# The chunked gated delta rule: the second value head with its two batches exchanged between the halves of the partitions

## The reference, cut to what matters

```
q,k,v,z = x @ W_qkvz;  q,k,v through a causal convolution of 4 taps and silu;  q,k normalized
attn    = inverse of (1 + strictly lower part of (beta k k^T * decay))          # 64x64 per chunk
v_prime = attn @ (v beta) - (attn @ (k beta exp g)) @ state
out     = (q exp g) @ state + (lower part of q k^T * decay) @ v_prime
state   = state * exp(g_last) + (k decay)^T @ v_prime                          # 128x128
result += rmsnorm(out * silu(z)) @ W_out[head]
```

## Time and profile before

| | |
|---|---|
| median of 3 runs | 4948.56 us (4940.16 to 4948.61) |
| the profiled execution | 4963.24 us, its span 4961.4 us |
| granted clock of PE, mean | 0.984 |
| PE busy | 4639.9 us, 94% |
| DVE busy | 3576.3 us, 72% |
| ACT busy | 3063.8 us, 62% |
| POOL busy | 693.1 us, 14% |
| DMA | 305.22 MB, 62 GB/s |

### The profile page before, as it was taken

How to read it: one execution, slowest core, us unless ns; L and a number is a source line. 1 busy time by engine, 2 the same in 40 slices (tenths; PEclk the granted TensorE clock), 3 DMA queues, 4 the chain that set the end, 5 groups by cost and what they waited for, 6 DMA issues and landing times.

```text
span 4961.4 us, 144941 instructions
## 1 busy us (share of the span) xinstructions
PE 4639.9 (94%) x54288; PEld 3178.9 (64%) x54320; DVE 3576.3 (72%) x7576; ACT 3063.8 (62%) x7979; POOL 693.1 (14%) x680
## 2 busy tenths in 40 slices
PE   4898999999999899999999899999999999999998
PEld 2555666666666566666666666666666666666666
DVE  7554777777777677777777677777777777777776
ACT  2333666666666566666666566666666666666665
POOL 0000111111111111111111111111111111111111
PEclk8999999999999999999999999999999999999999
DMA  2111222222223222222223222222223232222221
GB/s 61 32 43 60 66 69 52 61 67 61 68 50 81 69 68 50 64 67 61 59 58 81 68 58 59 64 63 65 60 57 81 68 69 55 59 66 60 69 58 34
DMA packets 760100, 305.22 MB, mean 62 GB/s; under 512 B 672880, under 2 KB 716016, under 8 KB 749168
## 3 DMA queue, kind: packets, MB, share of 16 engines
q1 hardware_dynamic: 620144, 287.40, 23.6%
q10 hardware_dynamic: 139264, 8.42, 1.8%
HBM read 216.96 MB, written 66.07 MB: 57 GB/s over the span
## 4 chain that ended last, share of the span: by engine, by line
PE 71%; DVE 8%; ACT 6%; issue 6%; SPq 5%; DMA 4%; ACTq 0%; DVEq 0%; POOL 0%; POOLq 0%
PE pj L660 16%; PE dsb L819 8%; PE pj L655 7%; PE pod L803 4%; PE pot L777 4%; PE dsb L791 4%; PE ms L693 4%; PE pot L748 4%; PE pod L760 3%; PE pj L650 3%; ACT arena L983 2%; PE pot L605 2%; PE ms L673 2%; SPq L333 2%; PE ms L687 2%
## 5 line engine op out<-in xcount | busy, mean ns | idle before, releaser
L660 PE MATMUL pj<-xnT,wt 128*128 128x512 f32 x2048 | 1023.2, 623 | 29.3 <-DMA cw<-in_L_attn_conv_weight 15.7
L1292 DVE SCALAR_TENSOR_TENSOR cy<-xpad,cw,cy 128x1024 f32<-128x1024 f32 x768 | 981.3, 1278 | 10.4 <-ACT cy L1003 1.2
L1562 POOL TENSOR_TENSOR rout<-rin,expo 128x2 f32<-128x2 f32 x512 | 358.3, 700 | 3743.4 <-DVE rin L1443 3743.4
L819 PE MATMUL dsb<-wo,yT 128*128 128x256 f32 x2048 | 575.7, 404 | 17.9 <-issue 16.9
L660 PEld LDWEIGHTS pj<-xnT,wt 128*128 128x128 f32 x2048 | 352.2, 192 | 358.9 <-issue 343.9
L1429 DVE SCALAR_TENSOR_TENSOR st<-st,gel,dsb 128x128 f32<-128x128 f32 x1536 | 430.4, 343 | 207.7 <-PE dsb L791 202.8
L1002 ACT ACTIVATE xpad<-pj 128x512 f32<-128x512 f32 x512 | 304.9, 596 | 360.8 <-PE pj L660 360.8
L655 PE MATMUL pj<-wt,xnT 128*128 128x256 f32 x2048 | 510.0, 392 | 0.0
L1062 ACT ACTIVATE yT<-dsb 128x256 f32<-128x256 f32 x512 | 202.2, 395 | 491.2 <-PE dsb L810 489.5
L819 PEld LDWEIGHTS dsb<-wo,yT 128*128 128x128 f32 x2048 | 348.7, 190 | 123.2 <-issue 95.4
L655 PEld LDWEIGHTS pj<-wt,xnT 128*128 128x128 f32 x2048 | 368.9, 190 | 84.0 <-issue 44.3
(11 more groups left out here) (174 smaller groups left out, 8011.6 us busy)
## 6 DMA issues: line engine op xcount, KB each, us to landing
qge<-ge_rows SPq DMA_DIRECT2D x64, 1024.0 KB, 7.4
wt<-in_L_attn_W_qkvz SPq DMA_DIRECT2D x64, 768.0 KB
gb<-g_rows SPq DMA_DIRECT2D x128, 256.0 KB
a_d<-at SPq DMA_DIRECT2D x64, 512.0 KB, 2.6
wo<-in_L_attn_W_out SPq DMA_DIRECT2D x64, 256.0 KB, 2.7
x_d<-xpair SPq DMA_DIRECT2D x128, 128.0 KB, 1.8
ap_<-a_d SPq DMA_DIRECT2D x512, 16.0 KB, 1.8
dd<-x_d SPq DMA_DIRECT2D x512, 16.0 KB, 2.1
```

Source lines behind the costliest of these rows:

```text
L660: last = mm(pj[n % 2][:, :], wt[:, k, col:col + DH], batch(xnT, k, i), start=(k == 0), stop=(k == KD - 1))
L819: last = mm(dsb[:, 0, GRP * DH:GRP * DH + D], yT[:, h, :], wo[:, p, h, :], start=(h == 0), stop=(h == GRP - 1))
L1292: stt(y, x[:, :, tap:tap + SEQ], cw[:, kind, tap:tap + 1], y, ALU.mult, ALU.add).then_inc(S["conv"], 1)
L1562: tt(rout[:, :], rin[:, :], expo[:, 0, 0:GRP], ALU.pow).then_inc(S["routs"], 1)
```

## The change

**PE.** The second value head (h = 1) holds its batches exchanged: batch b lies in the half `home(b, h)`, which is b for h = 0 and 1 - b for h = 1. The four products of S and of I then lie on the four different 64x64 tiles, since what is read lies in one half and what is written in the other for h = 1. K becomes four products of 128 columns instead of two of 256. The tiles of PSUM are laid out anew, as parts of one tensor `quad` of four banks: `po` over banks 0 and 1, `pw` (S) over 1 and 2, `pks` (K) in 2, `pstate` (U) over 2 and 3, `pyt` (R) in 3, `pod_rows` (O) in 0. I of chunk 7 waits for `accs` as well, and the wait for `og` of the head before goes from I of chunk 0 to the start of chunk 0.

**The inverse.** All four products of a round read from one half and write where they should: r = 0 reads `ee` alone, and so PE doesn't wait for the `eturn` DMAs there; DVE does, in `add_round(0, 1)`. `negated` copies the three tiles in another order.

**ACT.** `output_columns` puts the exchanged columns back: two copies of 128x128 instead of one of 128x256. vt: each tile is emptied with four copies of 128x128 instead of two of 128x256 (16 per head, not 8). z: one silu of 128x256 and two of 64x256 for each tile instead of one of 128x512; and of the tile of chunks 0 and 1 the first of these is moved from slot 4 to slot 2, right behind `decay_exp`.

**DVE, POOL, layouts.** Units are numbered u = h·8 + c instead of c·2 + h; `kn`, `kn2` and `qe` hold a column per head, with two small DVE instructions more in each of `coefficients` and `query_eps`, and L1558 on POOL works on 128x16 instead of 128x8. v1's batches are put into the convolution exchanged. The state's update stays on VectorE, with its source in `pstate`.

```
+        def home(b, h):
+            return b if h == 0 else 1 - b
...
                 if r == 0:
                     loaded(pe, d_ee, g, GRP * NBLK)
-                    loaded(pe, d_et, g, GRP * NBLK)
-                    after(pe, "pneg", g, 2)
+                    after(pe, "pneg", g, 3)
...
-                for b in range(NB):
-                    last = mm(pkw[half(b), 0:GRP * DH], kq[:, p, c, b, :],
-                              st[:, c % 2, b, :, :].rearrange("p h d -> p (h d)"), start=True, stop=True,
-                              tile_position=(0, b * CH))
+                for h in range(GRP):
+                    for b in range(NB):
+                        last = mm(pks[half(b), h * DH:(h + 1) * DH], kq[:, p, c, home(b, h), :],
+                                  st[:, c % 2, home(b, h), h, :], start=True, stop=True, tile_position=(0, b * CH))
...
-                for h in range(GRP):
-                    for b in range(NB):
-                        rhs = rr[half(b), h, :] if c else vb[p][half(b), h, :]
-                        last = mm(pkw[half(b), (GRP + h) * DH:(GRP + h + 1) * DH], bda[half(b), p, c * GRP + h, :],
-                                  rhs, start=True, stop=True, tile_position=(b * CH, b * CH))
+                for a in range(NB):
+                    for h in range(GRP):
+                        rhs = rr[half(a), h, :] if c else vb[p][half(a), h * NC, :]
+                        last = mm(pw[half(home(a, h)), h, :], bda[half(a), p, h * NC + c, :], rhs,
+                                  start=(c == 0 or h == 1), stop=True, skip_group_check=True,
+                                  tile_position=(a * CH, home(a, h) * CH))
...
-                    for v in range(2):
-                        c = 2 * i + v
-                        last = fn(vb[p][:, c * GRP:(c + 1) * GRP, :].rearrange("p h d -> p (h d)"),
-                                  src[:, v * GRP * DH:(v + 1) * GRP * DH], ACT.Copy, scale=kn[:, c:c + 1])
+                    for v in range(4):
+                        c, h = 2 * i + v // GRP, v % GRP
+                        last = fn(vb[p][:, h * NC + c, :], src[:, v * P:(v + 1) * P], ACT.Copy, scale=kn[:, h, c:c + 1])
                 elif kind == "z":
-                    last = fn(zz[p][:, 2 * i:2 * i + 2, :, :].rearrange("p c h d -> p (c h d)"), src[:, :], ACT.Silu)
+                    z = src[:, :].rearrange("p (c h d) -> p c h d", c=2, h=GRP)
+                    if part != 1:
+                        last = fn(zz[p][:, 2 * i:2 * i + 2, 0, :], z[:, :, 0, :], ACT.Silu)
+                    if part != 0:
+                        for b in range(NB):
+                            last = fn(zz[p][half(1 - b), 2 * i:2 * i + 2, 1, :], z[half(b), :, 1, :], ACT.Silu)
...
-                fn(yT[:, :, :].rearrange("p h t -> p (h t)"), dsb[:, 1, GRP * DH:2 * GRP * DH], ACT.Copy
-                   ).then_inc(S["yte"], 1)
+                for b in range(NB):
+                    dst = bass.AP(tensor=whole.tensor, offset=whole.offset + b * CH,
+                                  ap=[list(whole.ap[0]), [DH + (CH if b == 0 else -CH), GRP], [1, CH]])
+                    last = fn(dst, rows[:, :, b, :], ACT.Copy)
...
                 if s == 2:
                     decay_exp(g)
+                    empty_ring(g, p, 2, 0)
...
-                add = eturn[:, :, :] if (r, n) == (1, 1) else ee[:, us, :]
+                if (r, n) == (0, 1):
+                    loaded(dve, d_et, g, GRP * NBLK)
+                add = eturn[:, :, :] if n and r != 1 else ee[:, us, :]
```

More of the change, by code:

```diff
@@ L818, in out_project @@
                 for h in range(GRP):
-                    last = mm(dsb[:, 0, GRP * DH:GRP * DH + D], yT[:, h, :], wo[:, p, h, :],
-                              start=(h == 0), stop=(h == GRP - 1))
+                    last = mm(pod_rows, yT[:, h, :], wo[:, p, h, :], start=(h == 0 and not bank_cleared),
+                              stop=(h == GRP - 1), skip_group_check=True)
                 last.then_inc(S["od"], 1)
@@ L933, in column_stage @@
                 for b in range(NB):
-                    fn(colstage[half(b), :, i, :].rearrange("p k (c h) -> p k c h", h=GRP),
-                       src[:, b], ACT.Copy).then_inc(colev, 1)
+                    dst = colstage[half(b), :, i, :].rearrange("p k (h c) -> p k c h", h=GRP)
+                    if i < COLS - 1:
+                        last = fn(dst, src[:, b], ACT.Copy)
+                    else:
+                        for h in range(GRP):
+                            last = fn(dst[:, :, :, h], src[:, home(b, h), :, :, h], ACT.Copy)
+                    last.then_inc(colev, 1)
             def aside(q, t, place):
@@ L970, in _, with empty_ring @@
                     aside(q, t, 2)
-            def empty_ring(g, p, n):
+            def empty_ring(g, p, n, part=None):
                 kind, i = ring[n]
```

125 lines of the change are left out of this document (67 added, 58 removed).

## The result

| | before | changed |
|---|---|---|
| median | 4948.56 us (5 runs, 4935.20 to 4953.43) | 4974.86 us (5 runs, 4963.56 to 4978.56) |
| ratio to before | 1 | 1.0053 (95% interval 1.0038 to 1.0069) |
| profiled execution | 4963.24 us, span 4961.4 | 4963.56 us, span 4961.8 |
| mean granted clock | 0.984 | 0.982 |

The changed kernel is slower by half a percent, 26 us, or 0.4 us per head. I had forecast 4903 us and 0.9% less; the range 4830 to 4960 doesn't hold it. The rival "ACT's added work decides" said 4973.

A forecast was written before the change was run, and what follows sets the result against it. PE, busy 94%, was taken to bound the kernel but be held by other engines at four places per head. Legs -0.2 - 0.45 - 0.1 + 0 = -0.75 us, 60 heads, -45 us: 4903 us from 4948.56; range 4830 to 4960.

The forecast's parts named there:

- ACT's added work decides: Rival: vt copies, table load and z on ACT delay DVE's mean squares at both head ends; 4973 us, chance 0.16.
- S and I halve: S and I on PE go from four rounds to two, -0.2 us each, 205 us of PE work in all.
- The rival without it: Rival: four products don't run together, S and I stay at 0.58 us; 4940 us, chance 0.14.
- K costs nothing: K on PE as four products of 128 columns: taken as 0, between -13 us and as much the other way.
- Most of PE's gain is off the path: Little of PE's 205 us is on the path, since PE waits for another engine at four places of a head.
- L1 to U of chunk 2, -0.2: From the first sums of squares (L1) to U of chunk 2, PE without a hold, one S: -0.2 us per head.
- U of chunk 2 to r1, -0.45: From U of chunk 2, past second sums of squares (L2), to the inverse's second round (r1): -0.45 us, between -1.0 and 0.
- -0.95: Removing PE's eturn wait: mean square of chunk 6 to second round falls from about 8.5 to 7.6 us, -0.95.
- +0.15 at most: DVE's two added small query_eps instructions, at 0.08 us or less each, delaying the mean square of chunk 6.
- +0.35: z tile in three instructions behind the ee DMAs on ACT, delaying chunk 6's mean square: +0.35 us, between 0.1 and 0.54.
- r1 to K1, -0.1: Second round to next head's K of chunk 1 (K1): -0.1 us, between -0.55 and +0.4; ACT's vt copies +0.7 until the squares.
- K1 to L1, 0: K of chunk 1 to first sums of squares, table load and part of z ahead of squares: 0, between -0.2 and +0.4.

The follow-up runs named there:

- the run with four rounds: Changed kernel with four more products with a matrix of zeros in every S and I, restoring PE's work: 1.0130 of before, +38 us to the changed kernel.
- their repairs: Changed kernel with VectorE emptying the last of four vt tiles: 1.0027 of before; changed kernel with second table load and first part of z behind chunk 0's squares: 0.9977.
- whose repair: Changed kernel with the three query_eps instructions moved behind piece 11, into VectorE's wait for PE: 0.9992 of before, -30 us to the changed kernel.
- the last vt tile: Changed kernel with the last of the four vt tiles emptied by VectorE in one multiplication, ScalarE emptying three: 1.0027 of before, -13 us to the changed kernel.
- three alone: Changed kernel with, singly, query_eps moved earlier, last vt tile on VectorE, table load and part of z behind the squares: -30, -13 and -38 us to it.
- 123 together with one row moved: Changed kernel with query_eps and an inversion row earlier, last vt tile on VectorE, table load and part of z behind the squares: 4851.60 us, 0.9804 of before.
- the run with three whole ones: Kernel before with query_eps made three instructions, the two added being 128x8 and writing spare columns: 0.9996 of before.

## Why the prediction was wrong

- **S and I halve.** Right: 0.38 us instead of 0.58, 0.20 each. The rival without it falls, and with it the page's rule on row tiles and banks (the Trainium skill, TensorEngine Tiling (Array Packing), Gotcha 1: PSUM Pressure), as far as time goes: both row tiles write both banks of `pw` and the rounds are two.
- **K costs nothing.** Right: K to Q is 0.46 us in the same timeline (Q starts at 3182.79), 0.48 before (3195.11 to 3195.59).
- **Most of PE's gain is off the path.** Right, shown by the run with four rounds: 38 of 191 us.
- **L1 to U of chunk 2, -0.2.** Right, -0.20.
- **U of chunk 2 to r1, -0.45.** This is the first step that failed: measured -0.03, namely -0.22 up to L2, where I had given nothing, and +0.19 behind it. The term that was mis-sized is the removal of the wait, "-0.95": from the mean square of chunk 6 to r1 it brought 0.55 us, 8.20 instead of 8.75, where my sum for DVE's way had said 7.6; and with the wait put back r1 is only 0.23 later and the time the same within the intervals. I had also left out that the first round now waits for ACT's third negated copy (20.0 us in all). The two costs against it were both too low. The small instructions of `query_eps`, "+0.15 at most", cost 0.49: I had taken the 0.08 us between overlapping starts of short instructions for what a short instruction costs, and had not looked whether the engine has a gap there. It has none for 7 us. The z tile, "+0.35", costs 0.58. That the mean square of chunk 6 is late by only 0.52 us against U of chunk 2, just the 0.5 that I had set, is luck: the costs are twice that, and some of it is taken up on the way.
- **r1 to K1, -0.1.** The second step that failed, by as much: +0.34, near the bound of +0.4. The +0.7 on ACT was the right size (DVE waits 2.15 instead of 1.46). But I took the mean of one head with slack and one without; K waits for the state in 49 heads, so that the head without slack was the ordinary one.
- **K1 to L1, 0.** Right as a sum, +0.04, and so partly by luck, since I was blind to its parts: z in three instructions +0.39 (8.61 against 8.22), the pull -0.90, its place ahead of the squares +0.55.
- **The table load.** The Trainium skill (ScalarE: Activation LUTs, What ACT_TABLE_LOAD costs) has a drain of 1380 ns with each switch; the changed kernel's rows have 1.29 us from the load to the silu again, and no drain.
- **The rival.** "ACT's added work decides" gave 4973 us, and 4975 was measured. The agreement of the sums flatters it: it put +0.4 into the leg from K1 to L1, where +0.04 was measured. Its two places, vt and the table load, are real, and their repairs bring 13 and 38 us. But `query_eps` on DVE, whose repair brings 30 us, is not in it.

The profiled execution of before was 14.7 us over the median of its runs, and I subtracted that. It plays no part in the miss.

## What to carry to other kernels

A gain on the busiest engine is worth what its waits leave of it; before pricing it, walk the order of the other engines between two waits and mark where each of them has no gap, since half a microsecond put there counted nearly fully here (30 us over 64 heads), and put a few pieces earlier, into a wait of the same engine, it was free. When a large change moves nothing, don't discard it: find the holds that took its gain and repair them together, since a repair alone can lose a part at the next hold (0.34 of 0.53 us with the last vt tile; 81 us for three alone, 123 together with one row moved). And when a cost is tested alone in the kernel before, check in the trace that it is the same cost: three whole instructions took 0.15 us more than one, the two halves and one whole 0.48.

## What the runs showed of the hardware that I had not expected

- Short instructions of VectorE for the two halves of the partitions don't overlap as whole ones do. One of 128x8 cost 0.07 us between two others (3225.32 to 3225.39), and in the run with three whole ones each adds 0.07; with two of 64x8 ahead of it, written to the other half, the three start 0.18 us apart, the first 0.45 us behind the accumulation and not 0.33, and the stretch is 0.49 us longer.
- Two silus of 64x256 to the other half of the partitions take 0.77 us together, 0.39 each, as long as one of 128x256, and don't overlap with the one before (3226.55, 0.39 us, then 3226.95); copies of 128x128 with a scale go at eight in 2.18 us, one every 0.25.
- Four products of 64x64 on the four tiles, with both row tiles writing the same two banks in different halves, run together: their eight passes start as two groups of four, each within 0.02 us, 0.16 us apart (3184.63 and 3184.79), and the next step starts 0.38 us behind the first. On two tiles they start in pairs, and it is 0.58 us.
